# Spare products without a reader in three places of a graph network kernel, on one Trainium2 core

## The reference

```
# layer 0, graph part: batch norm over the nodes
h = concatenate([h_fwd, h_bwd], axis=-1)              # two halves of 128 columns
mean = h.mean(axis=0); var = square(h - mean).mean(axis=0)
h = relu((h - mean) * rsqrt(var + eps) * gamma + beta)

# layer 1, linear attention: 8 heads of 64, k and v normalised per row
dots = einsum('bhnd,bhne->bhde', k, v)                # one 64x64 matrix per head
out = einsum('bhnd,bhde->bhne', q, dots) / N ; out = out @ w_out.T + b_out

# layer 1, slice attention: 8 heads, 64 slices
x_mid = x @ W_x + b_x ; fx_mid = x @ W_fx + b_fx      # split into 8 heads
slice_weights = softmax((x_mid @ W_slice + b_slice) / temp)
slice_token = einsum('bhnc,bhng->bhgc', fx_mid, slice_weights)
```

## Time and profile before

| what | value |
|---|---|
| time, three executions | 1757.81, 1766.34, 1767.80 us |
| median | 1766.34 us |
| profiled execution, its own time | 1758.78 us |
| its span, first to last instruction | 1757.0 us |
| TensorE products busy | 1648.6 us (94%) |
| VectorE busy | 962.0 us (55%) |
| mean granted TensorE clock | 0.981 |

### The profile page before, as it was taken

One profiled execution on the slowest core, in us unless ns is written; L12 is line 12 of the kernel. 1 busy time (PEld: TensorE's weight loads), 2 busy tenths in 40 slices (PEclk: granted clock), 3 DMA queues, 4 the chain that ended last, 5 costly groups with the idle time before them and its releaser, 6 DMA issues. The chain is left out here.

```text
span 1757.0 us, 31367 instructions
## 1 busy us (share of the span) xinstructions
PE 1648.6 (94%) x9423; PEld 1080.9 (62%) x9424; DVE 962.0 (55%) x2833; ACT 668.9 (38%) x1360; POOL 242.4 (14%) x290
## 2 busy tenths in 40 slices
PE   6889999998999899999998999999997989998988
PEld 5344556666667323333666999999864558644657
DVE  8999999997478663346422000000156864346962
ACT  3123445772134575665322444444322423101220
POOL 2000000002010004900072000000062111400103
PEclk9999999999999999999899999999998989999999
DMA  3001122337450000000526022122130002140001
GB/s 88 0 15 60 62 81 82 133 132 244 140 168 1 1 1 1 1 1 1 196 87 221 19 78 101 66 69 78 55 94 25 1 1 100 61 149 31 1 1 62
DMA packets 86411, 118.88 MB, mean 68 GB/s; under 512 B 6788, under 2 KB 72510, under 8 KB 86176
## 3 DMA queue, kind: packets, MB, share of 16 engines
q1 hardware_dynamic: 80992, 106.53, 18.1%
q0 software_dynamic: 3936, 10.37, 1.9%
q10 hardware_dynamic: 1376, 0.66, 0.1%
HBM read 70.66 MB, written 46.87 MB: 67 GB/s over the span
## 5 line engine op out<-in xcount | busy, mean ns | idle before, releaser
L657 PE MATMUL bank<-onehot_key,onehot_low 128*128 128x320 bf16 x1304 | 223.6, 301 | 20.0 <-DVE onehot_low L450 13.7
L446 DVE TENSOR_SCALAR onehot_key<-iota_keys,edge_keys 128x640 bf16<-128x640 f16 x652 | 231.5, 384 | 9.1 <-PE bank L657 4.4
L2002 ACT ACTIVATE hidden<-bank,b_cols 128x128 f32<-128x128 f32 x344 | 126.3, 367 | 175.7 <-PE bank L1900 152.3
L657 PEld LDWEIGHTS bank<-onehot_key,onehot_low 128*128 128x128 bf16 x1304 | 99.3, 98 | 133.3 <-DVE onehot_key L446 64.0
L2109 DVE TENSOR_TENSOR slot_columns<-bank,b_rows 128x256 f32 x43 | 18.3, 425 | 287.0 <-PE bank L1906 287.0
L1900 PEld LDWEIGHTS bank<-slot_columns,w 128*128 128x128 f32 x1376 | 161.7, 194 | 4.2 <-issue 2.2
L1900 PE MATMUL bank<-slot_columns,w 128*128 x1376 | 162.6, 277 | 1.3 <-ACT slot_columns L2010 1.3
L1906 PE MATMUL bank<-w,hidden 128*128 128x256 f32 x688 | 155.6, 379 | 0.0
L1906 PEld LDWEIGHTS bank<-w,hidden 128*128 128x128 f32 x688 | 127.5, 190 | 15.5
L523 ACT ACTIVATE edge_low_shifted<-edge_low,window_offset 128x631 f32 x81 | 66.7, 823 | 177.7 <-DVE onehot_low L450 176.0
L1616 ACT ACTIVATE XT<-bank 128x512 f32<-128x512 f32 x160 | 84.4, 602 | 60.6 <-PE bank L1544 60.6
(11 more groups left out here) (529 smaller groups left out, 2753.3 us busy)
## 6 DMA issues: line engine op xcount, KB each, us to landing
AT_dram<-at_strip SPq DMA_DIRECT2D x20, 640.0 KB, 4.8
A_dram<-a_strips SPq DMA_DIRECT2D x20, 640.0 KB, 3.1
sg_strip<-AT_dram SPq DMA_DIRECT2D x20, 640.0 KB, 3.9
back_strip<-A_dram SPq DMA_DIRECT2D x24, 480.0 KB, 7.3
w<-in_L_ffn_W1p SPq DMA_DIRECT2D x8, 1024.0 KB, 5.4
w<-in_L_ffn_W2p SPq DMA_DIRECT2D x8, 1024.0 KB, 7.9
slot_rows<-ty_zero SPq DMA_DIRECT2D x1, 6144.0 KB, 25.3
slot_columns<-slot_rows SPq DMA_DIRECT2D x12, 512.0 KB, 8.7
```

Of the source, the lines that this page charges most:

```text
L446: dve.tensor_scalar(ohk[:, q, :], ioh[:, :], key[:, ds(chunk(n, offset, q), 1)], None, ALU.is_equal).then_inc(s_key[q], 1)
L657: last = pe.matmul(bank[2 * (x % 2) + h][:, 0:HB], ohl[q // 2][:, :, q % 2], ohk[:, q, h * HB:(h + 1) * HB], start=False, stop=q == Q - 1, ...
L2002: act.activation(hid[:, f, 0:P], bank[f % 4][:, 0:P], ACT.Gelu, bias=b1[:, ds((e + 1) * FB + f, 1)]).then_inc(s_rg, 1)
```

## The change

TensorE gets products whose results nobody reads. Each multiplies `onesf` with something that already lies in SBUF, writes 512 columns of a bank that is free at that time, and neither waits for nor signals anything. They stand at three places: in `backward_stage` 3 before the last `back_columns` and 4 before `squares(1)`; in `linear_attention_stage` 6 before the last `dots` and 4 before the wait for `DT`; in `slice_stage` 10 between the turning of the two late tiles and the first `sums`.

```
--- before.py
+++ after.py
@@ -840,8 +840,14 @@
                                 last.then_inc(s_sum[0], 1)
                             if j == 4:
                                 squares(0)
+                        def keep_going(n):
+                            for _ in range(n):
+                                pe.matmul(bank[5][:, :], onesf[:, :], spread(onesf[:, :], 1, WT), start=True, stop=True)
+
                         back_columns(last_cut - 1)
+                        keep_going(3)
                         back_columns(last_cut)
+                        keep_going(4)
                         squares(1)
 
                     @block.scalar
@@ -2263,15 +2269,22 @@
                                                  start=False, stop=t == T - 1, skip_group_check=True)
                             last.then_inc(s_use, 1)
 
+                        def keep_going(n):
+                            for _ in range(n):
+                                pe.matmul(bank[7][:, :], onesf[:, :], wc[:, 0, 0:W], start=True, stop=True)
+
                         for t in range(T):
                             if t + DEEP - 1 < T:
                                 kv(t + DEEP - 1)
+                            if t == T - 1:
+                                keep_going(6)
                             dots(t)
                             if t == 3:
                                 pe.wait_ge(s_wq, 1)
                                 for c in range(CB):
                                     last = pe.matmul(bank[7][:, 0:C], onesf[:, :], wsq[:, c, :], start=c == 0, stop=c == CB - 1)
                                 last.then_inc(s_wn, 1)
+                        keep_going(4)
                         pe.wait_ge(s_dt, 1)
                         for p in range(IB):
                             last = pe.matmul(bank[p][:, 0:C], DT[:, p, :], wo[:, p, :], start=True, stop=True)
@@ -2503,6 +2516,8 @@
                             for k in range(2):
                                 last = pe.transpose(bank[4 + h][:, k * P:(k + 1) * P], XN[:, REST[0] + k, h * P:(h + 1) * P], ident[:, :])
                         last.then_inc(s_tr, 1)
+                        for _ in range(10):
+                            pe.matmul(bank[3][:, :], onesf[:, :], wf[:, 0, :], start=True, stop=True)
                         for t in range(T):
                             if t == 0:
                                 pe.wait_ge(s_free, 1)
```

## The result

The change makes the kernel a little slower. The median of 20 executions is 1767.91 us against 1763.33 us for 20 of the kernel before. The ratio is 1.0028, with a 95% interval of 1.0016 to 1.0040. At 1763 us that is +4.9 us, between +2.8 and +7.1. The forecast was -1.8 us. The median lies inside the stated range of 1755.5 to 1772 us, but the time moved the other way. The interval is 0.12% to either side, so this measurement tells far smaller differences than the 0.5% that the prediction allowed for.

The account below looks back on a forecast made before the run. Chains of small steps after TensorE's waits ran at 1.2 GHz in three places, so only half-pace products could pay. Terms -1.27 - 2.35 + 1.83 = -1.8 us took the median 1766.34 to 1764.5 us, range 1755.5 to 1772.

Parts of the forecast that it names:

- The terms at the places: Time changes forecast at each place: batch norm -1.27 us, linear attention -2.35 us, slice opening +1.83 us.
- The price of a spare record: All three places: 0.43 us per record of 512 float32 columns at 2.4 GHz; a spare product is two records, 0.86 us.
- The signs that the prediction named for being right: PEclk 1.00 at three places, four TensorE waits gone, squares 1.3 and projection 2.35 us sooner, first sums 3.3 us later.
- What follows shifts with TensorE: Behind the linear attention: the later work moves with TensorE, so the -2.35 us carries through.
- So all of it is on the path: Batch norm's end: only VectorE's fold and the block's end follow, so the whole -1.27 us counts.
- The delay goes through to the end: Slice loop: TensorE bounds it, waiting only 1.6 us in all, so the opening's +1.83 us isn't absorbed.
- The size of the gain: Gain from half-pace products at the places, with 6.83, 13.66 and 6.83 us at 1.2 GHz; net sum -1.8 us.
- Rival A: All three places: ordinary executions have no clock falls there, so spares are pure overshoot, +8.0 us, 1774.3 us; chance 0.08.
- waits of 3 to 5 us: Argument that the three clock falls follow waits of this length, which every execution has.
- Rival B: All three places: spares don't hold the clock, which falls at the same instants; +12.2 us, 1778.5 us; chance 0.04.
- Rival C: The same places: falls cost more than profiled, and the change removes that too; 1757.0 us, -0.53%; chance 0.09.
- The overshoot: Spares outlasting their waits: 0.65 us and later in batch norm, 1.85 + 1.3 in linear attention, 3.3 in slice opening.

Follow-up runs that it names:

- e7: The change plus six spare products in the waits of the slice stage's tail, against the kernel before: ratio 0.9989, -1.9 us.
- e8: The kernel before with only six spare products, in the waits of the slice stage's tail: ratio 0.9984, -2.8 us.
- e5: The kernel before with only 8 spare products, in the slice opening: ratio 0.9987, -2.3 us.
- e11: The kernel before with 8 spare products in the slice opening and 2 in the middle of the slice loop: ratio 1.0023, +4.1 us.
- e3: The kernel before with only the slice opening's 10 spare products: ratio 1.0042, +7.4 us.
- e10: The change itself, timed again against the kernel before: ratio 1.0036, +6.3 us.
- e12: The kernel before, unchanged, profiled a second time: one execution of 1761.05 us.
- e6: The change with smaller batches (batch norm 2 + 3, linear attention 3 + 2, slice opening 5), against the kernel before: ratio 0.9976, -4.2 us.
- e4: The kernel before with only 6 spare products, in the slice opening: ratio 1.0005, +0.9 us.
- e9: Smaller batches (2 + 3, 3 + 2, 5) at the three places plus six spare products in the slice tail, against the kernel before: ratio 0.9953, -8.3 us.

## Why the prediction was wrong

**The terms at the places were right, for the one profile they were read from.** -1.27, -2.35 and +1.83 us were forecast, and the profile shows -1.26, -2.26 and +1.86. The price of a spare record was 0.43 us: (8.75 - 0.59) / 19 in the slice opening. A product with `onesf` on both sides costs the same: (2.74 - 0.59) / 5. The signs that the prediction named for being right came too: PEclk 1.00 in all three places, no idle time left ahead of the readers, and the first tile's sums 3.3 us later. They all look at the places alone, and the loss came from elsewhere.

**"What follows shifts with TensorE" failed.** That step took everything behind a place as shifted and otherwise unchanged. The products behind it did shift, but the clock's falls did not shift with them. The Taylor stage's opening got a fall (+1.7 us), and the slice tail got a long one (+4.2 us). Taking the tail's falls away brought the changed kernel from +4.9 or +6.3 to -1.9 us (e7), of which some 2.8 is there without the change too (e8). Why the fall in the tail is long after the change is argued, not shown; e5 against e11 speaks for the tail's place in time. "So all of it is on the path" was true of the 1.27 us and not the whole story.

**"The delay goes through to the end" was right and too small.** The 1.83 us went through: the loop took 74.17 us in both profiles. Of the +7.4 us that the slice part costs by itself, 1.8 is this. Its profile (e3) has 5.6 more in the tail and the last projection, but the execution that it shows took no longer than before's (1758.83 and 1758.78 us), so it can't account for the +7.4.

**The size of the gain was read from one profile.** I credited each execution with falls of 6.83, 13.66 and 6.83 us, 27.3 in all. The timed runs of e10 show 9.3 us less at the lower level, not 27.3. In unchanged code the linear attention had 6.8 us in e3 and e8, and the slice opening 3.4 in e12. Rival A stood on this. It was given 0.08 and +8.0 us, and was right in part: overshoot costs 0.8 us net in e3's linear attention instead of winning 2.3. An estimate from the two: the 8.0 us of overshoot that rival A worked out, less 9.3 us at 0.42 (the slope of the runs of before on e10's chip), is +4.1 us, where +6.3 was measured with +3.5 in its interval. Rival A's own condition, that the falls are gone altogether, didn't hold in any profile. The Trainium skill (TensorE: Matmul & The Clock Gate, section "What's actually happening") warns against fitting a model to one count of products at the lower level. The runs agree: one and the same linear attention had 13.66 and 6.8 us, the slice opening 6.83 and 3.41. I should have weighed it as more than a far rival. Against rival A the prediction also held waits of 3 to 5 us; the batch norm's were 1.76 and 2.30.

**Rival B is refuted**: PEclk is 1.00 through all batches. **Rival C too**: nothing in the median was won.

**The overshoot was seen and its meaning was not.** The working had 0.65 + 0.9 us in the batch norm, 1.85 + 1.3 in the linear attention and 3.3 in the opening. e6 against e10, on different chips, puts some 10 us on leaving it out, uncertain by 4.

What stays open: how often the kernel before has the long fall in its tail, so how much of the measured +4.9 us is that; why e3 costs 6.5 us more than e4; and whether the untouched stages in the middle, which took longer in both profiles of the changed kernel than in any profile with the batch norm as before, owe that to the change. No kernel was run that adds the same products where they change neither a wait nor the clock, so an effect of the added instructions themselves isn't excluded.

## What to carry to other kernels

Spare products held TensorE's clock wherever they stood, but each batch should end before its wait does: count records times their pace against the idle time ahead of the reader, and leave one out rather than add one. Judge such a change by timed runs with their mean clock, and not by the falls in one profile. Look past the place for the next chain of small steps, since the clock may fall there instead; with that covered too, e9 was the fastest kernel here, 8.3 us below before.

## What the runs showed of the hardware

- The granted clock fell at different instants for the same code. In the slice opening it fell 1.2 us into a wait of 5.09 us in one profile of the kernel before, and 4.5 us into it in another, with 6.83 and 3.41 us at 1.2 GHz.
- The clock stayed at 1.2 GHz for 10.2 us although TensorE was busy 9.23 of them (the changed kernel's windows row at 1708.7). First came products of 128 columns, then a wait of 0.97 us and six records of 512 columns that took 4.71 us instead of 2.84.
- The spread of a kernel's times goes with the clock. On three chips the kernel before took 1752.5 to 1764.3, 1750.4 to 1765.2 and 1755.8 to 1767.7 us, with 0.48, 0.52 and 0.42 us of time for each us at the lower level.
